# Four-layer graph network: panels of block 0 multiplied last, node blocks taken up by single groups, low one-hots compared with numbers in PSUM, and the wait for stored blocks moved into the loop

## What is computed

```python
dst = (12500 * uniform(200000) ** 2).astype(int32); order = argsort(dst); src, dst = src[order], dst[order]

h = maximum(layernorm(x), 0)                       # layer 0: a weight for each of 16 edge types
x = x + segment_sum(einsum('ni,rio->rno', h, W)[etype, src], dst) + bias + h @ loop_weight
h = maximum(layernorm(x), 0)                       # layer 1
x = x + concat([h, segment_sum(h[src], dst)], 1) @ W1.T + b1
h = maximum(layernorm(x), 0)                       # layer 2: an MLP on each edge, mean over the edges
m = relu(concat([h[src], h[dst], edge_attr], 1) @ Wa + ba) @ Wb + bb
x = x + segment_sum(m, dst) / maximum(degree, 1) + h @ Wn + bn
h = maximum(layernorm(x), 0)                       # layer 3
x = x + concat([h, segment_sum(concat([h[src], edge_attr], 1) @ Wc + bc, dst)], 1) @ Wd + bd
```

## Time and profile before

| | us |
|---|---|
| time before, median of 3 runs | 7200.89 |
| lowest and highest of the runs | 7191.73, 7232.2 |
| the profiled execution's own time | 7163.53 |
| its span in the trace | 7161.7 |
| layer 0, from 265 us | 2446 |
| layer 1 | 926 |
| layer 2 | 2703 |
| layer 3 | 822 |

### The profile page before, as it was taken

How to read it: one execution, slowest core, us unless ns; L and a number is a source line. 1 busy time by engine, 2 the same in 40 slices (tenths; PEclk the granted TensorE clock), 3 DMA queues, 4 the chain that set the end, 5 groups by cost and what they waited for, 6 DMA issues and landing times. The chain is left out here.

```text
span 7161.7 us, 86379 instructions
## 1 busy us (share of the span) xinstructions
PE 4714.0 (66%) x24800; PEld 3020.3 (42%) x24815; DVE 2438.5 (34%) x6392; ACT 2060.6 (29%) x3761; POOL 3998.2 (56%) x4125
## 2 busy tenths in 40 slices
PE   6565665666676656888646666666666666668885
PEld 3343443333333332344435554455545555533433
DVE  6443343333443333434222222222222222234232
ACT  5333333333566550010112222222222222210000
POOL 0466666666666555655246665555555555546653
PEclk8656567677666677888667887777777777778886
DMA  5433333332333335655222222222222222245562
GB/s 212 148 70 71 73 77 77 78 80 76 103 105 110 99 98 178 210 199 199 66 54 63 64 64 60 61 62 60 59 59 58 60 59 58 60 144 203 191 206 74
DMA packets 626790, 724.54 MB, mean 101 GB/s; under 512 B 235557, under 2 KB 526858, under 8 KB 607084
## 3 DMA queue, kind: packets, MB, share of 16 engines
q1 hardware_dynamic: 427578, 506.86, 21.5%
q0 software_dynamic: 130976, 185.66, 11.7%
q10 hardware_dynamic: 67986, 28.96, 1.5%
HBM read 518.59 MB, written 201.58 MB: 101 GB/s over the span
## 5 line engine op out<-in xcount | busy, mean ns | idle before, releaser
L1117 POOL DMA_INDIRECT layer_msg<-snd_table,layer_idx x1565 | 1480.3, 946 | 1305.7 <-DMA rel_table<-first_rows 442.8
L1128 POOL DMA_INDIRECT layer_msg<-rel_table,idx_rel x1536 | 1556.7, 1013 | 840.0 <-issue 420.9
L1811 PE MATMUL layer_sum_ps<-layer_sel,layer_msg 128*128 128x128 f32 (+14 forms) x8192 | 1139.7, 292 | 986.3 <-issue 445.8
L1835 PE MATMUL layer_unit_ps<-layer_frame_hot,layer_low_hot 128*128 128x350 bf16 (+9 forms) x3792 | 1111.5, 440 | 758.9 <-ACT layer_frames L1348 425.6
L1811 PEld LDWEIGHTS layer_sum_ps<-layer_sel,layer_msg 128*97 128x97 f32 (+2 forms) x8192 | 1069.4, 209 | 1161.1 <-issue 638.6
L1348 ACT CAST layer_frames<-layer_unit_ps 128x700 fp8e4<-128x700 f32 (+9 forms) x1268 | 953.1, 785 | 1341.0 <-remote 539.0
L1128 POOL DMA_INDIRECT layer_msg<-h_table,idx_src x896 | 849.9, 949 | 658.5 <-issue 238.5
L1851 PE MATMUL layer_panel_ps<-layer_piece,layer_pairs 128*128 128x504 fp8e4 (+9 forms) x3920 | 953.8, 399 | 124.6 <-issue 84.5
L1835 PEld LDWEIGHTS layer_unit_ps<-layer_frame_hot,layer_low_hot 128*128 128x128 bf16 x3792 | 395.3, 124 | 1310.4 <-issue 614.0
L1522 DVE TENSOR_TENSOR layer_msg<-layer_pre_ps,layer_msg 128x512 f32<-128x512 f32 x392 | 270.3, 690 | 1128.6 <-remote 696.0
L1851 PEld LDWEIGHTS layer_panel_ps<-layer_piece,layer_pairs 128*128 128x128 f16 x3920 | 391.2, 103 | 622.1 <-issue 253.5
(11 more groups left out here) (236 smaller groups left out, 3780.6 us busy)
## 6 DMA issues: line engine op xcount, KB each, us to landing
layer_piece<-counts SPq DMA_DIRECT2D x48, 1575.0 KB
layer_attr<-in_edge_attr_dram SPq DMA_DIRECT2D x790, 64.0 KB
rel_table<-first_rows SPq DMA_DIRECT2D x98, 512.0 KB, 2.7
layer_piece<-counts SPq DMA_DIRECT2D x24, 1500.0 KB
layer_piece<-counts SPq DMA_DIRECT2D x16, 1593.8 KB
layer_rcv<-rcv_table SPq DMA_DIRECT2D x396, 64.0 KB
layer_msg<-snd_table,layer_idx POOLq DMA_INDIRECT x1565
layer_piece<-counts SPq DMA_DIRECT2D x16, 1543.8 KB
```

Source lines behind the costliest of these rows:

```text
L1117: nc.gpsimd.indirect_dma_start(msg[g][:, u, 0:2 * D if dense else width], None, of, bass.IndirectOffsetOnAxis(ap=idx_slot[g][:, u:u + 1], ...
L1128: nc.gpsimd.indirect_dma_start(msg[g][:, u, 0:2 * D if dense else width], None, of, bass.IndirectOffsetOnAxis(ap=idx[:, at:at + 1], axis=0 ...
L1811: last = nc.tensor.matmul(sum_ps[g % 2][0:sums, 0:span], msg[g][:, u, c0:c1], sel[j][:, u, 0:span], start=n_part == 0, stop=n_part == len( ...
L1835: last = nc.tensor.matmul(unit_ps[unit % 2][:, half * 512:half * 512 + cols], low_hot[k % HOT][:, 2 * (r % 2) + v, :], frame_hot[j][:, v, ...
```

## The change

It does four things.

1. `BLOCK_ENDS` is written in groups, rounded up to single groups instead of to iterations of 8; the setup's checks follow (two VectorE operations on small tiles take another form).
2. `SEQUENCE` multiplies panels 3 to 19 first and panels 0, 1, 2 (the first 92 groups) last, in layers 1 and 3. Blocks 1 to 7 no longer wait for panels 0 to 2; block 0 waits for all.
3. `low_hot` is compared with `window_iota` in PSUM instead of `iota` in SBUF.
4. The wait for `stored` moves from ahead of `run` into `nodes`, behind the loop set-up and the last 8 groups. Layer 2 uses the same function and gets the wait too.

The schedule of parts becomes: layers 1 and 3: 1 (20), 2 (28), 8 (33), 9 (43), 3 (48), 4 (53), 10 (58), 5 (64), 11 (69), 6 (74), 7 (79), 12 (84), 0 (89); the static code ends at step 94 instead of 100. Layer 0: block 12 at groups 379 to 383. The frames of panels 0, 1 and 2 (84, 56, 44) are added in steps 72 to 83 instead of 4 to 15; those of panels 3, 4 and 5 (38, 36, 30) in steps 4 to 15.

```diff
-BLOCK_ENDS = (14, 19, 23, 27, 30, 33, 35, 38, 40, 42, 44, 46, 48, 49)
+BLOCK_ENDS = (107, 151, 184, 212, 237, 259, 279, 298, 316, 333, 349, 364, 379)
@@
+LATE = 3
+SEQUENCE = list(range(LATE, len(PANELS))) + list(range(LATE))
+LATE_GROUPS = PANELS[LATE][0]
@@
-            first_step[b] = (BLOCK_ENDS[b] - FIRST) * PER
+            first_step[b] = BLOCK_ENDS[b] - FIRST * PER
@@
-                ends = min(BLOCK_ENDS[b] * PER, DENSE_1)
-                ready = PIECES * (2 + min(k for k, panel in enumerate(PANELS) if panel[0] + panel[1] >= ends))
+                ends = min(BLOCK_ENDS[b], DENSE_1)
+                needed = [k for k, n in enumerate(SEQUENCE) if PANELS[n][0] < ends and (b == 0 or n >= LATE)]
+                ready = PIECES * (2 + max(needed))
@@ load_piece, low_sums copy, combine, add_frames, multiply_piece
-                    _, ng, tiles, fw, at = PANELS[s // PIECES]
+                    _, ng, tiles, fw, at = PANELS[SEQUENCE[s // PIECES]]
@@ add_frames
-                                frame_base[0:1, bass.ds(frames_before[k] + t, count)], engines=[DVE_ENGINE],
+                                frame_base[0:1, bass.ds(at + t, count)], engines=[DVE_ENGINE],
@@ make_hot
-                            iota[:, :].unsqueeze(1).to_broadcast([P, TILES, P]), ALU.is_equal)
+                            window_iota.unsqueeze(1).to_broadcast([P, TILES, P]), ALU.is_equal)
@@
                 def nodes(b, m):
+                    dve.wait_ge(stored, 16 * stores * (static_blocks + 1))
@@
                     dve.wait_ge(shifted, 2)
-                    dve.wait_ge(stored, 16 * stores * (static_blocks + 1))
                 run(dve, DVE_ENGINE, edges, nodes, next_window)
```

More of the change, by code:

```diff
@@ L389, in _ @@
                 link(nc.vector.tensor_scalar(double[:, :], group_of[:, :], float(DOUBLE_1), None, ALU.is_lt))
-                count_from(lowest, BLOCK_ENDS[0] * PER, 1.0)
-                for end in BLOCK_ENDS[1:NB - 1]:
-                    count_from(lowest, end * PER)
+                count_from(lowest, BLOCK_ENDS[0], 1.0)
+                for end in BLOCK_ENDS[1:]:
+                    count_from(lowest, end)
                 link(nc.vector.tensor_scalar(lowest[:, :], lowest[:, :], float(BLK), None, ALU.mult))
                 count_from(outside, DENSE_1, float(N))
-                link(nc.vector.tensor_scalar(highest[:, :], outside[:, :], float(8 * BLK - P), None, ALU.add))
+                link(nc.vector.tensor_scalar(width_step[:, :], group_of[:, :], float(LATE_GROUPS),
+                                             float(BLK - 8 * BLK), ALU.is_lt, ALU.mult))
+                link(nc.vector.scalar_tensor_tensor(out=highest[:, :], in0=outside[:, :],
+                                                    scalar=float(8 * BLK - P), in1=width_step[:, :], op0=ALU.add,
+                                                    op1=ALU.add))
                 link(nc.vector.memset(any_bad[:, :], 0.0))
@@ L874, in layer_phase @@
             if b <= 7:
[L875 to L877 removed]
+                ends = min(BLOCK_ENDS[b], DENSE_1)
+                needed = [k for k, n in enumerate(SEQUENCE) if PANELS[n][0] < ends and (b == 0 or n >= LATE)]
+                ready = PIECES * (2 + max(needed))
+            if BLOCK_ENDS[b] > DENSE_1:
                 ready = max(ready, 1 + min(z for z in range(STEPS)
[L879 removed]
+                                           if DENSE_1 + groups_by[z] >= BLOCK_ENDS[b]))
             first_step[b] = ready
@@ L1047, in layer_phase @@
             frames_before = [0]
-            for _, ng, tiles, _, _ in PANELS:
+            for n in SEQUENCE:
+                _, ng, tiles, _, _ = PANELS[n]
                 frames_before.append(frames_before[-1] + ng * TILES // tiles)
@@ L1443, in _ @@
                         if z % PIECES == 0 and 0 <= k < len(PANELS):
-                            _, ng, tiles, fw, _ = PANELS[k]
+                            _, ng, tiles, fw, _ = PANELS[SEQUENCE[k]]
                             cols = ng * TILES // tiles * fw
@@ L1600, in add_frames @@
                 def add_frames(k, s):
-                    _, _, _, fw, _ = PANELS[k]
+                    g0, _, tiles, fw, _ = PANELS[SEQUENCE[k]]
+                    at = g0 * TILES // tiles if tiles == 2 else g0 * TILES - DOUBLE_1 * TILES // 2
                     begin, end = frames_by(k, s), frames_by(k, s + 1)
```

2 lines of the change are left out of this document (removed).

## The result

The changed kernel takes 7236.14 us (median of 20 runs, 7219.65 to 7263.67), the kernel before 7186.73 (20 runs, 7164.28 to 7232.2): ratio 1.0067, interval 1.0053 to 1.008, some 49 us slower. The forecast was 12 us faster, with "slower by over 0.5%" at 0.19. The time lies inside the range that was given, but it moved the other way.

The account below looks back on a forecast made before the run. No engine was full on average, but VectorE's frames set the pace of steps 4 to 15. Layer 1 -15.5, layer 3 +11.6, layer 0 -8 made -12 us on the 7200.9 median: 7189, range 7125 to 7240.

Parts of the forecast that it names:

- Early steps: Layers 1 and 3, steps 4 to 15: fewer frames, -9 and -7 us (bounds -18 and -14).
- Late steps: Layers 1 and 3, steps 68 to 79: returning frames occupy VectorE, +12 and +17 us.
- Blocks moved into the loop: Layers 1 and 3, panel loop: 10.2 blocks inside for 9, 0.8 of them priced here, +8 and +2 us.
- 10 a block: Layer 1's loop: one block's node work costs 10 us, from 28 steps with 5 blocks at 259.2 against 210.
- Tail and wait: Behind the loops: tail -20 and +2 us, earlier start after moved wait -6.5 and -2.4, layers 1 and 3.
- Block 12 and PSUM: Layer 0: block 12 taken up 5 groups earlier, -3 us; low one-hot compared from PSUM, shorter gathers, -5 us.
- the rule of the Trainium skill: Layer 0: VectorE with two SBUF inputs doesn't hold up making gather descriptors, so the PSUM operand gives 0.
- Rival 2: Layers 1 and 3: late frames do not fit, late steps +43 and +29; in all +37 us, 7238, chance 0.15.
- Rival 3: GpSimd sets layer 0's pace: PSUM operand gives -20 for -5, in all -27 us, 7174; chance 0.15.

## Why the prediction was wrong

The stretches side by side, in us; at the slow pace two traces of each kernel, each from another chip (the second of the changed kernel is from one whose kernel before runs 1% faster, with 456 us in steps 16 to 67 of layer 1 and 447 in those of layer 3), at the fast one a trace of each:

| stretch | forecast | slow before | slow after | fast before | fast after |
|---|---|---|---|---|---|
| layer 1, steps 4 to 15 | -9 | 108, 105 | 105, 97 | 104 | 76 |
| layer 1, steps 16 to 67 | +8 | 471, 471 | 553, 543 | 370 | 377 |
| layer 1, steps 68 to 79 | +12 | 122, 122 | 116, 116 | 78 | 115 |
| layer 1, tail | -20 | 100, 100 | 81, 80 | 89 | 80 |
| layer 1, from there on | -6.5 | 56, 57 | 48, 48 | 55 | 48 |
| layer 3, steps 4 to 15 | -7 | 110, 115 | 97, 100 | 104 | 77 |
| layer 3, steps 16 to 67 | +2 | 452, 457 | 465, 459 | 339 | 367 |
| layer 3, steps 68 to 79 | +17 | 104, 104 | 111, 118 | 78 | 107 |
| layer 3, tail | +2 | 58, 58 | 57, 54 | 48 | 56 |
| layer 3, from there on | -2.4 | 32, 33 | 31, 32 | 33 | 32 |
| layer 0 | -8 | 2462, 2480 | 2483, 2470 | 2090 | 2055 |

- **Early steps.** Right in sign, and right that VectorE was full. The bounds of -18 and -14 were too small for the fast pace (-27 in each layer), where TensorE, busy 73.5 of 76.5 us, sets the end of the gain. That GpSimd can't follow there was seen only as a limit of these steps, not as work that comes later.
- **Late steps.** The occupation of VectorE was counted nearly rightly: for steps 72 to 79 it gave 93 and 86 us, and they took 87 and 76. But what they take in the kernel before was put at two thirds of steps 68 to 79, 81 and 70; the trace has 73 and 71, so by this count the term of layer 1 was +20 and not +12. Measured: +14 and +5. In layer 1 steps 68 to 71, taken as unchanged, fell from 49 to 29 us, which is why steps 68 to 79 did not grow at the slow pace; other node parts stand there. At the fast pace steps 68 to 79 came to 115 and 107 us, from 78.
- **Blocks moved into the loop.** This is the step that failed. "10 a block" was a mean over the steps of the kernel before, and a mean of stalls: node parts that met a burst of gathers and others that didn't. In the changed kernel more of them met one (14 of 16 results late for 6 of 14), and the term of +8 measured +82, and +87 between two traces of one chip (543 and 456 us). The count of 0.8 block more was right; the price of a block was not, and it changed for all blocks of the loop. The trace of before had shown steps of 15 to 25 us every few steps; the sum priced them as if they would stay where they were. In layer 3 the term of +2 measured +12 at the slow pace, and +28 at the fast one, where the later gathers make it.
- **Tail and wait.** Right at the slow pace: -19 and -20 for -20 and -8 and -9 for -6.5 in layer 1; in layer 3 -1 to -4 for +2, and -1 for -2.4. At the fast pace the tails gave less: -9 in layer 1, +8 in layer 3.
- **Block 12 and PSUM.** What the PSUM operand gives at the slow pace can't be told from the forecast's -5 or from nothing; the rule of the Trainium skill (page "SBUF — State Buffer", section "Who interferes with whom") that would have made it nothing is contradicted by the mean gather, which fell from 1020 to 997 ns, and by 25 us at the fast pace. Block 12's 3 us can't be told from layer 0's scatter: two traces of each kernel at the slow pace give 2462 and 2480 us before, 2483 and 2470 after, where the forecast had -8.
- **Rivals.** Rival 2, slower by the late panels, had the right sign, and its time (7238 for 7236) was close by luck: it had the frames (42 us of the loss at the slow pace), but put +43 and +29 where steps 68 to 79 measured -6 and +7, and did not name the node parts of steps 16 to 67. Rival 3, GpSimd as the pace of layer 0, fits the fast pace (-25 for -20) and not the slow one.

## What to carry to other kernels

When work is moved in a loop whose steps vary from 6 to 25 us, a mean price per moved block is worth little: find out what the long steps wait for and whether the moved work will stand in them. When steps get shorter, count what another engine got done in them meanwhile: here some 20 gathers came later in each layer. A forecast of a saving must say which engine is full in the place that receives the work, not only in the one that loses it. Several edits in one change should be measured apart: here three of them made 1%, and the fourth ate nearly all of it at the fast pace and more than all at the slow one.

## What the runs showed of the hardware

- Chips differ: the same kernel took 5721 to 5729 us on three and 7114 to 7195 on two. Layer 2 alone takes 1999 us in a trace at the fast pace and 2709 in one at the slow pace. The granted clock (0.84 and 0.74 in the mean) goes with it. With three quarters of the gathers of layers 1 and 3 left out, a slow chip ran their panel loops in 608 and 568 us, where the fast ones take 580 and 549 with all gathers.
- On the slow chips, TensorE's results are taken up to 14 us late while GpSimd issues gathers back to back. In the first trace of the changed kernel the 14 late ones of steps 16 to 67 are taken 1.0 to 6.2 us after the run of gathers has ended, and they had been due about 3 us or more behind its start; in the second trace 12 of 13 are taken up to 3.3 us after it and one before. On a fast chip GpSimd issued over 200 gathers without a pause in such a stretch, and 4 of 14 results were late, by 5 us at most.
- A compare of VectorE with one input in PSUM takes as long as with both in SBUF (679 and 684 ns for 128x512), and the gathers beside it are shorter: the mean of 1536 gathers fell by 22 to 25 ns.
- Register loads are dear: the longest of VectorE's waits before a frame, 3.8 us, holds one load of 16 numbers, and the 8 to 5 numbers of a later step took 0.6 to 1.4 us.
